# A transformer layer on one core: tokens normalised on GpSimd a batch further ahead, and a rearranged start

## The reference

```python
# x: (8, 512, 256), all float32
xn = layernorm(x)                                  # over the last axis, no gain or bias
qkv = xn @ Wqkv + bqkv                             # Wqkv (256, 768), 16 heads of 16
scores = q k^T * 16**-0.5, masked to |i - j| <= 64
attention = softmax(scores) v @ Wout + bout
logits = xn @ router_w + router_b                  # 8 experts
gate = softmax over the two largest logits
moe = sum over experts of gate * (relu(xn @ w1[e] + b1[e]) @ w2[e] + b2[e])
return x + attention + moe
```

## Time and profile before

| What | Value |
|---|---|
| median of three runs | 1004.77 us (1004.72 to 1008.41) |
| the profiled execution | 1007.1 us, span 1005.4 us |
| PE busy in the span | 92% |
| DVE busy | 82% |
| ACT busy | 75% |
| POOL busy | 48% |
| TensorE's granted clock, mean | 0.977 |

### The profile page before, as it was taken

One profiled execution on the slowest core, in us unless ns is written; L12 is line 12 of the kernel. 1 busy time (PEld: TensorE's weight loads), 2 busy tenths in 40 slices (PEclk: granted clock), 3 DMA queues, 4 the chain that ended last, 5 costly groups with the idle time before them and its releaser, 6 DMA issues. The chain is left out here.

```text
span 1005.4 us, 27570 instructions
## 1 busy us (share of the span) xinstructions
PE 928.6 (92%) x7688; PEld 893.3 (89%) x7688; DVE 827.9 (82%) x2174; ACT 752.3 (75%) x2015; POOL 481.9 (48%) x680
## 2 busy tenths in 40 slices
PE   3999899998999999999966999999999999999993
PEld 2788789898989898989956999999999999999993
DVE  5876799987888887888836889898889898898994
ACT  3666798888989898989934777776777767777763
POOL 4000023244454545555423666665666665666665
PEclk9999899999999999999987999999999999999997
DMA  3889432624353535352414222222222232222210
GB/s 116 292 295 301 147 87 62 189 64 148 103 150 100 155 96 165 86 170 82 141 44 158 37 33 41 43 40 40 32 33 41 44 52 42 33 44 42 32 22 21
DMA packets 73990, 96.06 MB, mean 96 GB/s; under 512 B 15389, under 2 KB 48800, under 8 KB 73824
## 3 DMA queue, kind: packets, MB, share of 16 engines
q1 hardware_dynamic: 56640, 77.96, 25.5%
q0 software_dynamic: 17312, 17.67, 11.0%
HBM read 63.70 MB, written 35.53 MB: 99 GB/s over the span
## 5 line engine op out<-in xcount | busy, mean ns | idle before, releaser
L940 ACT ACTIVATE weights_qkv<-weights_qkv,low 128x256 f32<-128x256 f32 (+1 forms) x512 | 241.0, 484 | 1.5 <-DVE low L751 1.5
L1312 ACT ACTIVATE hid<-ps_experts,b_s 128x256 f32<-128x256 f32 x312 | 130.9, 473 | 126.8 <-PE ps_experts L1377 113.6
L1206 POOL DMA_INDIRECT out<-y,target x78 | 146.8, 1882 | 120.4 <-DVE y L1281 108.5
L1029 PE MATMUL ps_attend<-pt,v_m 128*80 128x256 f32 (+7 forms) x1536 | 187.5, 271 | 1.6
L762 DVE TENSOR_TENSOR pt<-ps_attend,pt 128x512 fp32r<-128x512 f32 (+1 forms) x256 | 158.4, 620 | 35.2 <-ACT pt L953 30.6
L1392 PE MATMUL ps_experts<-w_hi,h_hi 128*128 128x256 f32 x624 | 177.3, 284 | 0.0
L1377 PE MATMUL ps_experts<-xgt_hi,w_hi 128*128 128x256 f32 x624 | 174.6, 280 | 1.7 <-DVE xgt_lo L1242 1.7
L1377 PE MATMUL ps_experts<-xgt_hi,w_lo 128*128 128x256 f32 x624 | 174.8, 280 | 0.0
L1377 PE MATMUL ps_experts<-xgt_lo,w_hi 128*128 128x256 f32 x624 | 174.4, 279 | 0.0
L1029 PEld LDWEIGHTS ps_attend<-pt,v_m 128*80 128x80 f32 (+3 forms) x1536 | 171.2, 162 | 3.5 <-issue 3.5
L1392 PE MATMUL ps_experts<-w_hi,h_lo 128*128 128x256 f32 x624 | 173.9, 279 | 0.0
(11 more groups left out here) (163 smaller groups left out, 2138.2 us busy)
## 6 DMA issues: line engine op xcount, KB each, us to landing
weights_qkv<-in_w SPq DMA_DIRECT2D x15, 1024.0 KB, 5.4
qk_hi<-weights_qkv SPq DMA_DIRECT2D x16, 512.0 KB, 3.7
qk_lo<-weights_qkv SPq DMA_DIRECT2D x16, 512.0 KB, 4.5
q_st<-qk_hi SPq DMA_DIRECT2D x128, 64.0 KB
k_st<-qk_hi SPq DMA_DIRECT2D x128, 64.0 KB
weights_qkv<-in_x SPq DMA_DIRECT2D x8, 512.0 KB, 4.8
xn_rows<-weights_qkv SPq DMA_DIRECT2D x8, 512.0 KB, 5.5
k_st<-qk_lo SPq DMA_DIRECT2D x64, 64.0 KB
```

What stands on the lines that cost most here:

```text
L940: ins = act.activation(wt[:, ring, at_tile(i)], wt[:, ring, at_tile(i)], ACT.Exp, bias=low[:, ring, i:i + 1], scale=-1.0, accum_out=total[ ...
L1029: ins = pe.matmul(ps[0:rows, bank_o, o:o + z - a], v_m[:, ring, vv, t, 0:rows], w[:, a:z], start=(j == 0 and t == 0 and p == 0), stop=(j = ...
L1206: pool.indirect_dma_start(out_tokens, bass.IndirectOffsetOnAxis(ap=target[:, h:h + 1], axis=0), y[:, h], None, bounds_check=T - 1, oob_is_ ...
L1312: ins = act.activation(hid[:, n % 2, j], ps[:, bank_h[n], j * ROWS:(j + 1) * ROWS], ACT.Relu, bias=b1[:, ds(e * FC + 2 * n + j, 1)])
```

## The change

1. **Normalising moves to GpSimd.** Batch 0 stays on ACT (`norm_first`); `norm(b, ring)` on POOL does all others as `tensor_scalar` with `rstd` and `shift`: batch 1 ahead of its constants, batches 2 to 7 in a loop. ACT's `variance_root` and DVE's `inverse_root` are done for batch b + 2 instead of b + 1 and stand behind the v hi and v lo of m = DC (tile 2); those of batch 1 stand ahead of the loop.
2. **The start.** Wqkv has a semaphore of its own (`s_wqkv`). ACT splits it directly after the square root of batch 0 and normalises behind that; DVE takes the lo of each part as soon as its hi is there. Biases and router weights follow the norm.
3. **Clearing.** POOL starts its memsets of `q_st`, `k_st`, `v_m` when `rstd` and `shift` of batch 0 are there (`s_rstd`).
4. **SP's order.** The load of x, the store of xn and their waits stand at the head of a batch instead of between its two halves of q/k stores.
5. **DRAM layout.** `qk_hi` and `qk_lo` change from (batch, tile, partition, n) to (batch, half, partition, tile, n), so that a partition's two tiles of a half are one run of 4 KB.

```diff
@@ norm_project, sync @@
-                sp.dma_start(w_raw[:], g.Wqkv.rearrange("(c p) n -> p c n", p=P)).then_inc(s_w, 16)
+                sp.dma_start(w_raw[:], g.Wqkv.rearrange("(c p) n -> p c n", p=P)).then_inc(s_wqkv, 16)
...
                 def batch(b, par):
+                    if more(b, 1):
+                        sp.wait_ge(s_xn, b + 2 + START)
+                        sp.sem_inc(g.tick, 1)
+                        if more(b, 3):
+                            sp.wait_ge(s_x, 16 * b + 48 + START)
+                            sp.sem_inc(g.tick, 1)
+                            load(b + 3, 1 - par)
+                        sp.wait_ge(s_xnout, 16 * b + 16 + START)
+                        sp.sem_inc(g.tick, 1)
+                        store_xn(b + 1, 1 - par)
                     for half in range(2):
                         m = slice(half * DC, (half + 1) * DC)
                         sp.wait_ge(s_qklo, 4 * b + DC * half + DC + QK0)
                         sp.sem_inc(g.tick, 1)
                         for split, of in ((g.hi_dram, qk_hi), (g.lo_dram, qk_lo)):
-                            sp.dma_start(split[ds(b, 1), m].rearrange("b m p n -> (b p) m n"),
+                            sp.dma_start(split[ds(b, 1), half].rearrange("b p m n -> (b p) m n"),
                                          of[:, par, m]).then_inc(s_qkstore[par], 16)
-                        if half == 0 and more(b, 1):
...
@@ gpsimd @@
+                pool.wait_ge(s_rstd, 1 + START)
                 pool.memset(g.q_st[:].bitcast(F32), 0.0).then_inc(s_zero, 1)
...
+                def norm(b, ring):
+                    pool.wait_ge(s_rstd, b + 1 + START)
+                    pool.sem_inc(g.tick, 1)
+                    if not isinstance(b, int):
+                        pool.wait_ge(s_tr, 2 * b - 2 + START)
+                        pool.sem_inc(g.tick, 1)
+                        pool.wait_ge(s_xnout, 16 * b - 16 + START)
+                        pool.sem_inc(g.tick, 1)
+                    for t in range(TB):
+                        ins = pool.tensor_scalar(xn[:, ring, t, :], x[:, ring, t, :], rstd[:, t:t + 1],
+                                                 shift[:, t:t + 1], ALU.mult, ALU.add)
+                    ins.then_inc(s_xn, 1)
+
+                norm(1, 1)
                 pool.memset(g.band[:], 0.0)
...
+                with pool.Fori(1, B // 2) as pair:
+                    for par in range(2):
+                        norm(2 * pair + par, par)
@@ vector @@
-                v.wait_ge(s_whi, 3 + START)
-                v.wait_ge(s_bq, 2 + START)
+                v.wait_ge(s_whi, 1 + START)
                 v.scalar_tensor_tensor(out=w_lo[:, :, 0:D], in0=w_raw[:, :, 0:D], scalar=SCALE,
...
+                v.wait_ge(s_whi, 2 + START)
...
+                v.wait_ge(s_whi, 3 + START)
...
                 statistics(1, 1)
+                inverse_root(1)
+                v.wait_ge(s_bq, 2 + START)
...
-                        if m == 0 and more(b, 1):
-                            inverse_root(b + 1)
...
+                        if m == DC and more(b, 2):
+                            inverse_root(b + 2)
@@ scalar @@
                 variance_root(0)
-                norm(0, 0, True)
-                act.wait_ge(s_w, 64 + START)
+                act.wait_ge(s_wqkv, 16 + START)
                 act.activation(w_hi[:, :, 0:D], w_raw[:, :, 0:D], ACT.Copy, scale=SCALE).then_inc(s_whi, 1)
                 act.activation(w_hi[:, :, D:3 * D], w_raw[:, :, D:3 * D], ACT.Copy).then_inc(s_whi, 1)
+                norm_first()
+                act.wait_ge(s_w, 48 + START)
...
                 hi_of_tokens(0, 0)
+                variance_root(1)
...
-                        if m == 0 and more(b, 1):
-                            variance_root(b + 1)
-                        if m == 1 and more(b, 1):
-                            norm(b + 1, 1 - par)
...
+                        if m == DC and more(b, 2):
+                            variance_root(b + 2)
@@ build @@
-        g.hi_dram = nc.dram_tensor("qk_hi", (B, 2 * DC, P, N), F32).ap()
-        g.lo_dram = nc.dram_tensor("qk_lo", (B, 2 * DC, P, N), F32).ap()
+        g.hi_dram = nc.dram_tensor("qk_hi", (B, 2, P, DC, N), F32).ap()
+        g.lo_dram = nc.dram_tensor("qk_lo", (B, 2, P, DC, N), F32).ap()
...
-        g.hi_rows = g.hi_dram.rearrange("b (w c) (a h r) n -> b w c h r a n", w=2, h=2, r=DH)
+        g.hi_rows = g.hi_dram.rearrange("b w (a h r) c n -> b w c h r a n", h=2, r=DH)
```

More of the change, by code:

```diff
@@ L121, in norm_project @@
         lg = sb("lg", [P, TB, E])
+        s_wqkv = sem("s_wqkv", "sp")
         s_w = sem("s_w", "sp")
@@ L373, in hi_of_tokens, with norm_first @@
                         act.activation(xt_hi[:, ring, c], ps[:, bank_t[c], :], ACT.Copy).then_inc(s_hi, 1)
[L375 to L380, removed]
+                def norm_first():
+                    act.wait_ge(s_rstd, 1 + START)
                     for t in range(TB):
-                        ins = act.activation(xn[:, ring, t, :], x[:, ring, t, :], ACT.Identity,
+                        ins = act.activation(xn[:, 0, t, :], x[:, 0, t, :], ACT.Identity,
                                              bias=shift[:, t:t + 1], scale=rstd[:, t:t + 1])
@@ L1463, in build @@
         g.s_stack = [ctx.enter_context(nc.semaphore(f"s_stack{ring}")) for ring in range(2)]
-        g.hi_rows = g.hi_dram.rearrange("b (w c) (a h r) n -> b w c h r a n", w=2, h=2, r=DH)
-        g.lo_rows = g.lo_dram.rearrange("b (w c) (a h r) n -> b w c h r a n", w=2, h=2, r=DH)
+        g.hi_rows = g.hi_dram.rearrange("b w (a h r) c n -> b w c h r a n", h=2, r=DH)
+        g.lo_rows = g.lo_dram.rearrange("b w (a h r) c n -> b w c h r a n", h=2, r=DH)
         with ExitStack() as front:
```

## The result

Timed in turns, the changed kernel takes 1000.59 us (median of 8, 998.84 to 1003.43) and the kernel before 1007.74 us (median of 8, 1003.15 to 1009.37): a ratio of 0.9937, with a 95% interval of 0.9917 to 0.9958. (Ratios here compare the runs made in turns and leave out the few executions that took over 1.5% more than the fastest of their kernel, so they need not be the quotient of the medians.) That is 6.3 us less, with an interval of 4.2 to 8.4. The kernel before stood at 1004.77 us in the three runs of the prediction; against its new median the 1000.3 us forecast would have been some 1003.2. The absolute time thus fits better than the step of 4.5 us behind it.

A forecast was written before the change was run, and what follows sets the result against it. TensorE waited on ACT in each projection batch, with VectorE's queue 0.6 us behind being the bound. Batch 7 at 14.6 + 12.95 + 52.1 + 9.5 = 89.15 us instead of 93.70; 4.5 off 1004.77 gave 1000.3 us, range 996.5 to 1003.8.

The forecast's parts named there:

- Part 1, the start: Start of the projection: first matmul of batch 0 at 14.6 us, 3.55 us earlier, bounds 2.8 to 3.8.
- The rival that it does nothing: Start edit: ACT or Wqkv is later than thought, only 1.0 us is left, 1002.8 us; chance 0.04.
- GpSimd's price: Normalisation on GpSimd: four tensor_scalars per batch take 2.3 us, from 1.6 to 2.9, hidden with 7 us to spare.
- Part 2, a steady batch: Projection batches 1 to 5: 10.42 us each through VectorE's queue, bounds 10.2 to 10.6; TensorE's wait mostly moves to L452.
- Batch 6: Projection batch without statistics or root: TensorE-bound, 9.5 us.
- The rival of a TensorE-bound batch: Projection: batches 1 to 6 take 9.5 us, 10.0 us gained, 994.8 us; chance 0.14.
- Batch 0: First projection batch: 12.95 us against 12.08, 0.87 us lost; an earlier clock rise could return up to 0.8 us.
- The tail: End of the projection, SP's last stores: 0 given back, bounds 0 to 2 us, as the layout halves the pieces.
- The rival that the tail keeps part of the gain: End of the projection: SP's last store still held by the ring, 1001.5 to 1003.0 us; chance 0.18.
- GpSimd too slow: Normalisation: TensorE waits 4t - 7.0 us in six batches for tensor_scalars of t; 1018 us at 2.5 us; chance 0.06.
- The total: Whole kernel: 4.5 us off the median of 1004.77 us, giving 1000.3 us; forecast chance 0.58.
- within 0.5%: Whole kernel: change too small to tell from none, under 5.0 us; chance 0.61, against 0.33 faster and 0.06 slower.

The follow-up runs named there:

- e_start_only: The kernel before with only the new start (early Wqkv split, own semaphore, memsets behind the first root); 1008.76 us, ratio 1.0005 to the kernel before.
- e_root_late: The changed kernel with VectorE's root of batch b+2 moved behind the next tokens' lo; 1001.62 us, ratio 0.9925 to the kernel before.
- e_norm_x4: The changed kernel with GpSimd's normalisation of batches 1 to 7 done four times over; 1028.38 us in a single execution, beside 1013.17 for the kernel before.
- again_after: The changed kernel run once more, unaltered; 1007.74 us, ratio 0.9964 to the kernel before.
- e_old_layout: The changed kernel with q and k in DRAM by tile as before, in 2 KB pieces; 1012.03 us, ratio 1.0001 to the kernel before.

## Why the prediction came out as it did

- **Part 1, the start: right.** First matmul at 14.46 us, forecast 14.6. The root of batch 0 takes 0.17 us in its tensor_scalars, shift starts at 8.34 (done at about 8.5, as said), the normalisation at 8.67 (8.8), the transposes at 10.87 (11.0). The rival that it does nothing is out, by `e_start_only`.
- **GpSimd's price: right.** Forecast 2.3 us for four; measured 0.560 us each, 2.2 us. The prediction's estimate of 1.5 us from the Trainium skill (GPSIMD Engine Reference, "Elementwise — side-by-side cycle accounting") was too low by a third. The norm of batch 5 starts at 57.13 us and TensorE takes up its tokens at 63.81, 6.7 us later (7 forecast), so it is hidden.
- **Part 2, a steady batch: right.** Forecast 10.42 us for batches 1 to 5; measured 10.52, 10.50, 10.45, 10.49, 10.29, mean 10.45. The wait moved to the place named. Batch 6: 9.46, forecast 9.5. The rival of a TensorE-bound batch is out in this order of VectorE's queue, and `e_root_late` shows that it is the order: it runs at that rival's 9.5 us.
- **Batch 0: mis-sized.** Forecast 12.95 us; measured 12.13. The bound had been named (the clock might rise earlier, up to 0.8 us) and left out of the sum. The matmuls kept their slow length (0.63 us for 512 columns) until 18.03 us, 3.6 after the first matmul, where before they kept it until 23.88, 5.7 after it. (0.63 and 0.39 us are their lengths at a granted clock of 0.50 and 1.00 in `e_norm_x4`; in this stretch the profile shows 1.00 throughout, so that it is the clock is read from the lengths alone.) This term makes up 0.82 of the 0.85 us by which batch 7 was earlier than forecast: 88.30 against 89.15. In `again_after` it gave 0.3 us only, so the truth of it is a range.
- **The tail: 0, as taken, by a narrow margin.** SP's last store and VectorE's last addition end within 0.1 us of each other. The reason given, the bigger pieces, is shown twice: with 2 KB pieces 1.3 us are lost, now that the batches behind the first stack load take over 1 us less. The rival that the tail keeps part of the gain was a real mechanism that the layout just held off, and it took 1.7 us of `e_root_late`.
- **GpSimd too slow: out here**, with 2.2 us for four; how its price was wrong stands above.
- **The total.** The step is 5.4 and 4.9 us by the traces, 6.3 us (4.2 to 8.4) and 3.6 us (0.3 to 7.0) by the two timings, and 4.5 was forecast. The most weight went to "within 0.5%", the bound being 5.0 us. The first timing lies beyond it, the second within, and each interval holds it, so on which side of it the change falls is not shown. In the first trace the term of batch 0 makes the difference between 4.6 and 5.4 us. That the time itself came within 0.3 us of 1000.3 owes 3 us to the reference, which read 1004.77 in one set of runs and 1007.74 in the next.

What stays open: why the experts last 470 or 478 us at the same granted clock, and why the attention differs by up to 6 us among executions.

## What to carry to other kernels

When work leaves one engine, follow the queue of the engine that TensorE waits for next: here the gain of a batch was not the wait that vanished (1.04 us) but the 0.2 us that the VectorE order allowed, and putting one short chain behind the awaited instruction gave the other 1.0 us. A gain ahead of a stage's end only counts if the DMA issuer has slack there; look at who ends last, and by how little. Price lateness with the tightest batch, here the first, and with the clock that a pause costs, not with the steady batch alone.

## What the runs showed that I had not expected

- The same DMA issue on SP takes 0.34 to 0.43 us when few transfers are queued and 1.1 to 1.7 us behind the stack loads; with half as many pieces one of the two last issues became short (1.17 us in `e_old_layout`, 0.34 us in the kernel after; in the kernel before, with its longer batches, it took 0.38 us with 2 KB pieces).
- A VectorE tensor_scalar of 128x4 ends when GpSimd's running memset ends, whether that is 0.5 or 1.0 us later, and where memsets follow one another it can last through those that began after it (L308 of the kernel before, 8.47 to 10.34 us; the last memset ends at 10.31). Beside GpSimd's own tensor_scalars it took 0.27 to 0.49 us in `e_norm_x4`, instead of 0.17.
- TensorE's granted clock fell from 1.00 to 0.50 (matmuls of 0.63 instead of 0.39 us) with the pauses of 2.02, 2.44, 2.65 and 4.79 us for tokens in `e_norm_x4`, and not with the one of 1.58 us there or those of 0.65 to 0.88 us in the kernel after.
- With the granted clock at 1.00, TensorE began 870 matmuls between 700 and 800 us in one execution of the kernel after and 853 in another.
